# Queries loaded earlier, values taken from the keys' projection, and one transpose for the shift rows, in a fused attention and mixture-of-experts kernel

## The reference

```python
x = x + layernorm(attn(layernorm(x)))
x = x + layernorm(moe(layernorm(x)))

# attn: 8 heads in 2 groups of 4, head size 128, latent size 32
q = (x @ wq).reshape(B, T, 2, 4, 128)
k = einsum('bkhl,ld->bkhd', (x @ wk_down).reshape(B, T, 2, 32), wk_up)
v = einsum('bkhl,ld->bkhd', (x @ wv_down).reshape(B, T, 2, 32), wv_up)
scores = einsum('bqhrd,bkhd->bhrqk', q, k) * 128 ** -0.5
probs = softmax(where(causal, scores, min))
y = einsum('bhrqk,bkhd->bqhrd', probs, v).reshape(B, T, 1024) @ wo

# moe: 32 experts of inner size 64 (top 6, from 2 of 4 groups), a shared one,
# and one of 16 anchor experts of size 32; all are computed, then weighted
```

## Time and profile before

| | us |
|---|---|
| median of 3 runs | 406.68 |
| lowest and highest | 405.88, 409.79 |
| the profiled execution | 405.73 |
| its span, first to last instruction | 403.7 |
| PE, POOL, DVE, ACT busy | 384.1, 307.8, 277.7, 231.1 |

### The profile page before, as it was taken

How to read it: one execution, slowest core, us unless ns; L and a number is a source line. 1 busy time by engine, 2 the same in 40 slices (tenths; PEclk the granted TensorE clock), 3 DMA queues, 4 the chain that set the end, 5 groups by cost and what they waited for, 6 DMA issues and landing times.

```text
span 403.7 us, 6919 instructions
## 1 busy us (share of the span) xinstructions
PE 384.1 (95%) x2104; PEld 257.1 (64%) x2104; DVE 277.7 (69%) x707; ACT 231.1 (57%) x450; POOL 307.8 (76%) x366
## 2 busy tenths in 40 slices
PE   8988999997999999999989999999999999999992
PEld 8664555653454554445457878787878788788871
DVE  5994998672867893737329866568765677566764
ACT  4555355663556475755784555856664755675652
POOL 6117958997599999998999886599946997386651
PEclk9999999998999999999999999999999999999997
DMA  7358280071530310500000000000000000000000
GB/s 221 50 152 137 43 206 4 0 98 23 173 40 3 59 21 4 79 4 2 2 2 0 2 2 0 2 26 1 2 0 2 26 1 2 1 1 28 0 0 27
DMA packets 9907, 14.56 MB, mean 36 GB/s; under 512 B 1232, under 2 KB 5520, under 8 KB 9488
## 3 DMA queue, kind: packets, MB, share of 16 engines
q1 hardware_dynamic: 9584, 13.49, 16.5%
q10 hardware_dynamic: 288, 0.64, 0.5%
HBM read 6.26 MB, written 1.05 MB: 18 GB/s over the span
## 4 chain that ended last, share of the span: by engine, by line
PE 76%; POOL 7%; DVE 6%; ACT 4%; DMA 3%; issue 3%; SPq 1%; POOLq 0%; DVEq 0%; ACTq 0%
PE ps L1298 9%; PE ps L1391 9%; PE ps L1299 9%; PE ps L1300 9%; PE ps L1411 8%; PE ps L1424 8%; PE ps L1493 5%; PE ps L1494 4%; PE ps L1495 4%; DMA qst<-q_lo 3%; PE ps L1434 3%; POOL silu L940 2%; DVE nmax_h L1196 2%; PE ps L1444 2%; PE ps L1394 1%
## 5 line engine op out<-in xcount | busy, mean ns | idle before, releaser
L940 POOL TENSOR_TENSOR silu<-silu,cwb 128x512 f32<-128x512 f32 x80 | 102.3, 1294 | 33.9 <-ACT silu L1070 29.8
L1196 DVE TENSOR_REDUCE nmax_h<-ps 128x1 f32<-128x512 f32 (+3 forms) x152 | 91.8, 654 | 41.0 <-PE ps L1394 20.8
L854 POOL TENSOR_TENSOR probs<-probs 128x1024 f32<-128x1024 f32 (+3 forms) x64 | 106.4, 1691 | 15.6 <-ACT probs L1040 9.4
L1040 ACT ACTIVATE probs<-ps 128x512 f32<-128x512 f32 (+1 forms) x152 | 80.0, 578 | 59.9 <-PE ps L1411 44.7
L1262 DVE TENSOR_TENSOR ps<-silu,ps 128x512 f32<-128x512 f32 (+1 forms) x84 | 57.8, 694 | 26.8 <-POOL silu L940 25.7
L1269 DVE TENSOR_TENSOR h_lo<-ps,h_hi 128x512 fp32r<-128x512 f32 (+1 forms) x84 | 57.1, 685 | 21.7 <-ACT h_hi L1082 21.2
L1070 ACT ACTIVATE silu<-ps 128x512 f32<-128x512 f32 x80 | 47.6, 598 | 37.0 <-PE ps L1300 32.1
L1391 PE MATMUL ps<-kst,qst 96*128 96x512 f32 (+3 forms) x192 | 62.8, 389 | 5.0 <-issue 3.0
L1082 ACT ACTIVATE h_hi<-ps 128x512 fp32r<-128x512 f32 (+1 forms) x84 | 49.9, 597 | 30.2 <-DVE ps L1262 29.1
L1298 PE MATMUL ps<-xT_hi,w_hi 128*128 128x512 f32 x164 | 65.5, 399 | 0.1
L1411 PE MATMUL ps<-qst,kst 98*128 98x512 f32 (+1 forms) x152 | 62.8, 448 | 1.7 <-ACT probs L1040 0.8
(11 more groups left out here) (187 smaller groups left out, 509.1 us busy)
## 6 DMA issues: line engine op xcount, KB each, us to landing
qst<-q_hi SPq DMA_DIRECT2D x14, 256.0 KB, 5.4
qst<-q_lo SPq DMA_DIRECT2D x7, 256.0 KB, 6.7
x_sb<-in_attn_x SPq DMA_DIRECT2D x4, 256.0 KB, 6.4
raw<-in_ffn_w_gate SPq DMA_DIRECT2D x1, 1024.0 KB, 5.1
raw<-in_ffn_w_up SPq DMA_DIRECT2D x1, 1024.0 KB, 5.2
raw<-in_ffn_w_down SPq DMA_DIRECT2D x1, 1024.0 KB, 4.8
kst<-k_hi SPq DMA_DIRECT2D x6, 128.0 KB, 5.1
result<-x_sb SPq DMA_DIRECT2D x3, 256.0 KB, 2.3
```

The source lines that it names most:

```text
L854: nc.gpsimd.tensor_tensor(into, into, probs[:, BUF[n, kt], j:end, cols], ALU.add).then_inc(added, 1)
L940: nc.gpsimd.tensor_tensor(silu[:, k % HRING, :], silu[:, k % HRING, :], cwb[:, m % 2, t // ET, :], ALU.mult).then_inc(scaled_ready, 1)
L1040: nc.scalar.activation(probs[:, BUF[n, kt], j:j + w, at:at + cols], bank(full)[:, 0:w * cols].rearrange("p (w c) -> p w c", w=w), ACT.Exp) ...
L1196: nc.vector.tensor_reduce(nmax_h[:, n % 2, i, j:j + w, h], bank(full)[:, 0:w * keys].rearrange("p (w k) -> p w k", w=w), AX.X, ALU.max, ne ...
```

## The change

It changes steps and the planner together.

- **Values.** For chunks 1 to 3 `vproj` is gone. ACT copies rows 64 to 127 of `kproj`'s result (`vT_copy`) into the upper half of the buffer `k_hi`, which is twice as tall now; `v_turn` transposes it in four pieces on PE; `v_copy` follows as before. `kproj`'s bank stays taken until `vT_copy`. Chunk 0 keeps `vproj`.
- **Shift rows.** `nm2` holds part, head and tile in 32 adjacent columns, so `shift` is one transpose to 32 rows of 128; `shift_copy` copies 32 x 128 instead of 8 x 512, and `s_dma` moves pieces of 128 numbers instead of 512.
- **Ranks.** The chain of x, keys and values of chunk c goes from c + 1.5 to c + 0.9 (chunk 1: 2.2 to 1.4), a block's queries from n + 0.2 to n - 0.4. `load(0)` follows block 2's last query transfer instead of block 0's shift rows.
- **Costs.** Transfers of queries count 650 instead of 330 on their way, keys 350 and 400 instead of 220. Several PE steps get other costs. A change between the narrow steps (`pv`, `ones`) and the others costs 10 or 19 in the plan and lifts the rank, so that narrow steps are grouped.
- **Seed.** A number drawn from the step's index adds up to 0.04 to each rank.

```diff
+V_ROWS = slice(64, 128)
...
+TILED = ("pv", "ones")
+TILE_IN, TILE_OUT, TILE_STAY, TILE_SHY = 10, 19, 0.3, 0.5
+SEED, WOBBLE = 12, 0.04
-DMA_TRIP = {"q_hi_dma": 330, "q_dma": 330, "k_hi_dma": 220, "k_dma": 220, "s_dma": 160, "x_load": 200, "load": 800, "store": 200, "tail_store": 200}
+DMA_TRIP = {"q_hi_dma": 650, "q_dma": 650, "k_hi_dma": 350, "k_dma": 400, "s_dma": 190, "x_load": 200, "load": 800, "store": 200, "tail_store": 200}
...
+        k = len(self.steps) * 2654435761 + SEED * 40503
+        rank += WOBBLE * ((k ^ k >> 13) % 65536 / 65536)
...
+                    if engine == "PE":
+                        rank += 0 if (ev[0] in TILED) == tiled else TILE_STAY if tiled else TILE_SHY
...
+            if engine == "PE" and (ev[0] in TILED) != tiled:
+                tiled = not tiled
+                cost += TILE_IN if tiled else TILE_OUT
...
-        rank = 2.2 if c == 1 else c + 1.5
+        rank = 1.4 if c == 1 else c + 0.9
...
-        step("PE", ("kproj", c), 70, rank, ("xT_lo", c), ("wkv_split",), bank=1, until=("k_lo", c))
+        step("PE", ("kproj", c), 70, rank, ("xT_lo", c), ("wkv_split",), bank=1, until=("vT_copy", c))
...
-        step("PE", ("vproj", c), 140, rank + 0.3, ("xT_lo", c), ("wkv_split",), bank=1, until=("v_copy", c))
-        step("ACT", ("v_copy", c), 45, rank + 0.3, ("vproj", c))
+        step("ACT", ("vT_copy", c), 60, rank + 0.1, ("k_lo", c), c >= 2 and ("v_turn", c - 1))
+        step("PE", ("v_turn", c), 31, rank + 0.3, ("vT_copy", c), bank=1, until=("v_copy", c))
+        step("ACT", ("v_copy", c), 45, rank + 0.3, ("v_turn", c))
...
-        rank = n + 0.2 if n > 1 else SECOND
+        rank = n - 0.4 if n > 1 else SECOND
...
-        step("PE", ("shift", n), 60, n + 1, ("nm_split", n))
-        step("ACT", ("shift_copy", n), 60, n + 1, ("shift", n), n >= 2 and ("s_dma", n - 2))
+        step("PE", ("shift", n), 15, n + 1, ("nm_split", n))
+        step("ACT", ("shift_copy", n), 25, n + 1, ("shift", n), n >= 2 and ("s_dma", n - 2))
...
-        step("SP", ("load", a), 200, 2, ("s_dma", 0) if a == 0 else ("wsplit", a - 1, WSPLITS[-1]))
+        step("SP", ("load", a), 200, 2, ("q_dma", 2) if a == 0 else ("wsplit", a - 1, WSPLITS[-1]))
...
-        with nc.sbuf_tensor("k_hi", [GROUPS * LAT, CH], F32R) as k_hi, nc.sbuf_tensor("k_lo", [GROUPS * LAT, CH], F32R) as k_lo:
+        with nc.sbuf_tensor("k_hi", [2 * GROUPS * LAT, CH], F32R) as k_hi, nc.sbuf_tensor("k_lo", [GROUPS * LAT, CH], F32R) as k_lo:
             pass
+        vT = k_hi[V_ROWS].bitcast(F32)
...
-        nm2 = sb("nm2", [P, TPC, SHIFTS, REP], F32R)
-        shift_rows = sb("shift_rows", [SHIFTS * REP, 2, CH], F32R)
+        nm2 = sb("nm2", [P, SHIFTS, REP, TPC], F32R)
+        shift_rows = sb("shift_rows", [SHIFTS * REP * TPC, 2, P], F32R)
...
+                elif kind == "vT_copy":
+                    c = ev[1]
+                    act.wait_ge(lo_ready, LO["k_lo", c])
+                    if c >= 2:
+                        act.wait_ge(misc_full, MISC["v_turn", c - 1])
+                    nc.scalar.activation(vT[:], bank(("kproj", c))[V_ROWS], ACT.Copy).then_inc(copied, 1)
...
+                elif kind == "v_turn":
+                    c = ev[1]
+                    pe.wait_ge(copied, COPIED["vT_copy", c])
+                    bank_turn(pe, ev)
+                    for t in range(TPC):
+                        last = nc.tensor.transpose(bank(ev)[:, GROUPS * LAT * t:GROUPS * LAT * (t + 1)], vT[:, P * t:P * t + P], ident[V_ROWS, V_ROWS])
+                    last.then_inc(misc_full, 1)
...
-                    for i in range(TPC):
-                        last = nc.tensor.transpose(bank(("nm_split", n))[0:SHIFTS * REP, P * i:P * i + P], nm2[:, i].rearrange("p a j -> p (a j)").bitcast(F32), ident[:])
-                    last.then_inc(misc_full, 1)
+                    nc.tensor.transpose(bank(("nm_split", n))[0:SHIFTS * REP * TPC, 0:P], nm2[:].rearrange("p a j i -> p (a j i)").bitcast(F32), ident[:]).then_inc(misc_full, 1)
```

More of the change, by code:

```diff
@@ L349, in plan @@
                 if kt == last_of(n, f):
-                    step("PE", ("ones", n, f), 10 + (CH - first_col(n, f)) * 17 // 100, rank - 0.15, *(("add", n, kt, part) for part in range(len(PARTS))),
+                    step("PE", ("ones", n, f), (CH - first_col(n, f)) * 173 // 1000, rank - 0.15, *(("add", n, kt, part) for part in range(len(PARTS))),
                          f and ("ones", n, first_of(n, f - 1)), bank=0 if f else 1, until=("recip", n))
@@ L676, in bank_turn @@
                     engine.wait_ge(lo_ready, LO["k_lo", user[1]])
+                    engine.wait_ge(copied, COPIED["vT_copy", user[1]])
                 elif kind == "proj":
@@ L684, in bank_turn @@
                     engine.wait_ge(copied, COPIED["m_copy",])
-                elif kind == "vproj":
+                elif kind in ("vproj", "v_turn"):
                     engine.wait_ge(copied, COPIED["v_copy", user[1]])
```

54 lines of the change are left out of this document (30 added, 24 removed).

## The result

The changed kernel takes 405.9 us (median of 20 runs, 400.6 to 412.0), the kernel before 407.7 beside it on the same chip; the ratio is 0.989, 95% interval 0.985 to 0.993. By the ratio it is faster by 1.1%, about the least that can be told apart, where 3% was forecast. The spread of its runs goes with how long PE (called TensorE in the expectations) had its lower clock: those at a mean granted clock of 0.973 to 0.981 took 400.6 to 403.1 us, those at 0.959 to 0.965 took 405.7 to 407.8, and the two at 0.948 and 0.947 took 411.6 and 412.0. The profiled execution took 402.97 us with a span of 400.9, which is 2.8 us less than the 405.73 of before; all that follows compares profiled executions, unless a ratio or a median is given.

What follows compares the result with a forecast made beforehand. PE, busy for 95% of the span, was taken as the bound, with POOL nearly as full in the attention's later half. 405.7 - 9.1 - 4.5 - 1.2 - 1.5 + 1.0 + 2.6 = 393.0 us; range 389.0 to 400.0.

Steps and rivals of the forecast that it cites:

- PE's work: On PE before about 210 us: values 2.9, shift rows 2.4 and 18 fewer narrow groups 3.8, so 9.1 us less.
- Block 4's wait and the clock behind it: Before block 4's first scores: 2.95 us idle goes, plus 1.5 us of low clock after it, 4.5 us.
- Block 2: Block 2's queries land sooner, scores start at about 36 us: 1.2 us of PE idle and 1.5 us more saved.
- DVE's head start: Block 2's row maxima on DVE begin sooner; 1.5 us taken, bounds 0 and 3.9.
- What is added: New transfers, copies and first v_turn around block 0's shift rows and first exps cost 1.0 us, between 0 and 2.5.
- What POOL gives back: POOL can't start its first mul 15.3 us sooner, so 2.6 us of PE's gain is lost.
- the forecast's own least: Least POOL gives back: 15.3 us gained, less 11.7 of POOL's long waits and 3.0 of slack, 0.6 us.
- Rival 2: Waits for queries only move, another landing or the exps being late; only PE's work is gained, 396.6 us; chance 0.11.
- Rival 1: POOL bounds the attention's second half; only 6.4 us of its waits go, 399.3 us; chance 0.15.
- Rival 3: v_turn and the 32-column shift each cost a switch, 11 times, 2.3 us in all, 395.3 us; chance 0.07.
- Rival 4: ACT's early q_hi copies wait for landings and hold the exps; slower, 413.4 us at 3.4 us a copy; chance 0.04.
- Rival 5: Later weights load pushes POOL's splits, so PE waits for what it saved; only 1.7 us won, 404.0 us; chance 0.08.

Runs made afterwards that it cites:

- experiment 1: Changed kernel with block 1's shift rows issued ahead of block 3's queries in SP's list; 396.42 us profiled, ratio 0.976.
- experiment 5: The kernel of experiment 1 plus five matmuls with overwritten result on PE ahead of block 6's first row sums; 394.70 us profiled, ratio 0.971.
- experiments 9 and 10: The kernel of experiment 5 with chunks 1 to 3's values by their own matmuls (9), or shift rows turned by four transposes (10); medians 399.1 and 397.4 us.
- Experiment 12: Kernel before the change plus 12 matmuls with overwritten result in PE's wait for block 4's queries; 404.21 us profiled, ratio 0.996.
- Experiment 11: The kernel of experiment 5 with the first load of weights issued right behind block 0's shift rows, as before the change; 404.41 us profiled, ratio 0.991.
- experiment 8: The kernel of experiment 1 with POOL's adds of probabilities taking only the first half of their columns; 388.34 us, ratio 0.957.
- Experiment 2: Changed kernel plus 17 matmuls with overwritten result in PE's wait for block 1's shift rows; 399.54 us profiled, ratio 0.981.

## Why the prediction was wrong

The forecast was 393.0 us, and the profiled execution took 402.97, a median of 405.9. Of the 10.0 us between forecast and profiled execution, experiment 1 gives back 6.6 and experiment 5 another 1.7; the last 1.7 stay. By its own steps:

**PE's work, 9.1 us: right as far as it was measured.** On the page PE is busy for 8.4 us less, though longer at the lower clock. `v_turn` goes at the 0.36 us that four transposes took, and the two parts cost about 2.6 us each at the end of the kernel, where 2.9 and 2.4 were forecast (experiments 9 and 10). That a group switch costs 0.21 us, and 18 fewer save 3.8, was not run alone.

**Block 4's wait and the clock behind it, 4.5 us: right where it stands, and not enough.** Idle time and low clock are gone there. Experiment 12 gives the clock's 1.5 us by itself.

**Block 2, 1.2 and 1.5 us: right in direction.** The scores start at 35.97, forecast 36. Experiment 11 shows that without the load's new place the wait would have grown to 5.4 us; the term was priced by the old wait, and it protects more than that. The 1.5 us for DVE's head start was not tested.

**"What is added", 1.0 us: the step that failed.** It names what stands in front of block 0's shift rows on SP and ACT, and ends there. The same move puts block 3's queries in front of block 1's shift rows, one block later, and no term was there for it. Both facts were at hand: SP's order, in which `q_hi_dma` and `q_dma` of block 3 had moved past `s_dma` of block 1, and rows which show 7 us for a transfer that has others in front of it. The planner can't see it either: it gives a transfer of shift rows 1.9 us to land wherever it stands, so to it this order was free. Measured: 6.55 us by experiment 1, about half of it wait and half clock.

**What POOL gives back, 2.6 us: too small, by a slack that wasn't there.** The term counted 3 us of slack between POOL's first mul and PE's first down, the 6.3 us between them less 3.4 us of steps. None of it came out: the distance is 6.34 us before, 6.38 after, 6.39 in experiment 1 and 6.37 in experiment 5. Without the slack the forecast's own least is 15.3 - 11.7 = 3.6 us and not 0.6. With the shift rows in time, block 4's scores start at 85.3 us, 9.4 us sooner than before, and the first down comes 8.9 us sooner, where 15.3 less 2.6, so 12.7, was forecast; with experiment 5's filled wait it is 10.3, so 5.0 us of the 15.3 are given back or were never won. The first mul, at 201.68 there, is where the forecast had it (near 201), and the first down is not (208.05, forecast 206). The 1.4 us between experiments 1 and 5 come from the last stage of the attention, at 184 to 196 us, where PE waits for POOL and ACT and the clock can fall. POOL's idle time ahead of its adds, which was to shrink, was 15.6 us before and 15.2 in the changed kernel by the page's group, and 6.9 in experiment 1: these 8.7 us less are about the 8.9 us by which its first mul comes sooner there.

**The rivals.** Rival 2, another landing late in the place of the old one, is what happened; its price of 396.6 took the gain at the queries away and stopped there, without a low clock behind the new wait. Rival 1, POOL as the bound, gives some 6 us when half of each add is left out (experiment 8), so it costs something and isn't what sets the time. Rival 3, a switch in `v_turn` and in the 32-column shift, is refuted: the four turns take 0.36 us, and the step behind the shift starts 0.04 us after it (66.31 and 66.35). The rule that the prediction cites from the Trainium skill, TensorEngine Tiling (Array Packing), Key Properties, with 64x64 among the modes that its section Available Configurations lists, would make the turns pay a drain, and this row shows none. Rival 4's q_hi of block 3 did wait for a landing, 0.97 us, and started at 35.75; in experiment 1 it starts at 35.78, so this held nothing. Rival 5 is refuted as a mechanism, though its 404.0 is the nearest price to the measured time: the weights' splits begin at 42.06 us, and POOL never waited for the load.

With the one item moved and the one wait filled, the kernel takes 394.7 us, 0.4% above the forecast. The range ended at 400.0, under the measured time: it left out the prices of rivals 4 and 5, and none of the others had two stretches of low clock in it.

One thing stays open. The same waits in the last stage of the attention stand in the changed kernel, where the clock stays full around them, and in experiment 1, where it falls at 187.7 us:

```profile
194.24 0.79 PE L1446 MATMUL ps<-qst,kst 98*128 98x384 f32 x2 [0.42 <-ACT probs L1069]
...
196.01 1.07 PE L1469 MATMUL ps<-probs,ones 128*32 128x512 f32 x8 [0.98 <-POOL probs L875]
```

```profile
185.24 0.79 PE L1448 MATMUL ps<-qst,kst 98*128 98x384 f32 x2 [0.42 <-ACT probs L1071]
...
187.01 1.22 PE L1471 MATMUL ps<-probs,ones 128*32 128x512 f32 x8 [0.98 <-POOL probs L877]
```

Experiment 2 has them too (0.34 and 1.04 us), and the clock falls at 191. Experiment 5 shows that filling one of them keeps it up, not what decides between the two; nor was it found out why the clock falls at 67 us in experiments 9 and 10 and not in their base.

## What to carry to other kernels

When transfers are moved forward in a queue, list, for each small transfer that something waits for, what now stands in front of it, block after block and not only at the first. A few kilobytes behind 768 KB land as late as these do, and a planner with one landing time per kind will call that order free. Price a new wait of PE twice, once for the idle time and once for the low clock behind it, and price a wait that is removed by what it would have become after the other savings, not by its old length.
